# The second layer's score maximum from a difference and a positive part, and its denominator sum on one engine

## The chip, the cores and the metric

The kernel runs on one core of a Trainium2 chip. The metric is the device time of one execution in microseconds; lower is better. The engines are TensorE (PE in the profile, its weight loads PEld), VectorE (DVE), ScalarE (ACT), GpSimd (POOL) and SyncE (SP), which only issues transfers here.

## The reference

Two transformer layers over 2048 tokens of 128 features. The first has causal attention with 16 heads and a mixing by Fourier transforms; it is not touched. The second has a linear attention, not touched either, and then this attention over experts, with 8 heads, 5 experts and a head width of 64, of which the change touches the softmax:

```python
q = jnp.einsum('bthed,bthe->bhtd', q5, sd_g)
k = jnp.einsum('bthed,bthe->bhtd', k5, ss_g)
v = jnp.einsum('bthed,bthe->bhtd', v5, ss_g)
attn = jax.nn.softmax(jnp.einsum('bhid,bhjd->bhij', q * scale, k), axis=-1)
out = jnp.einsum('bhij,bhjd->bihd', attn, v)
o5 = jnp.einsum('bthd,dm->bthm', out, Wo).reshape(b, t, H, E, DIM)
return jnp.einsum('bthem,bthe->btm', o5, md)
```

`q5`, `k5`, `v5` are projections of the tokens per expert, `ss_g` and `sd_g` gates that keep the three best experts, `md` the mask of the three. Nothing is causal: each query sees 2048 keys.

## The kernel before

All work is written out by hand for each engine, with semaphores. The order of the second layer is one list, `SEQ1`, which `merge` makes from two: a foreground of 256 steps `u` (8 heads x 4 chunks of 512 queries x 8 pairs of key tiles), and a preparation of the next head whose items have a place in units of `u` (`preparation1`). Every engine walks this list and does its own part of each item, in order.

The foreground of a step is: `S`, TensorE computes the scores of two key tiles against a chunk of queries, transposed, into two PSUM banks (lines 775 and 776, two matmuls a tile: the second adds the fine part of the keys and, through a row of ones, minus the maximum of each query); ScalarE takes the exponential of both banks into `pbuf1` (line 960); two steps later `V` multiplies it with the values (line 786) and `D` adds it into the denominator sum `den`. `den` has 1024 columns; VectorE adds the first 704 of them (`SHARE`, line 1283; a copy in the first step of a chunk, line 1280), GpSimd the other 320 (lines 1383 and 1380). At the end of a chunk ScalarE copies the sum of products to `oT` (line 967), GpSimd adds the two halves of `den` (line 1388), TensorE folds and sums them (`F`, lines 797 and 802), VectorE divides (lines 1291 and 1292), and GpSimd multiplies with the expert mask into `onm` (line 1394) and adds that to `z` (line 1398). A step's exponential waits until the steps that used its buffer five steps ago are read.

The preparation of a head is: `w`, VectorE casts the weights (lines 1230 and 1231); `proj`, 48 projections of a token tile on TensorE (lines 747 to 749), each multiplied with the gates on VectorE (`gt`, line 1238) and, three of them together, summed over experts on GpSimd (lines 1367 to 1370), with two buffers for `gt`; `hi` and `lo`, the split into a coarse and a fine part (`sk1`, `sq1` by ScalarE, `sk2` and the rest of `sq1` by VectorE, lines 1250 and 1251); `t`, transposes (line 581) that ScalarE copies to `k1T`, `k2T`, `q1T`; and `max`: for each of 16 query tiles, four matmuls of 512 keys (line 759), each reduced by VectorE to one number a query (line 1256). `m` takes the largest of the four and its negative goes into `sq2`; `q2` transposes that into the row that `S` reads. So the maxima of a chunk must be done before its scores.

PSUM has eight banks. Four hold scores, one the products, and three (4, 5, 7) are the ring: `proj`, `max`, `F`, `y`, `t`, `q2` and `zt` take them in turn. `Ring` records for each item its turn and which engine reads it, and `take` lets TensorE write turn n only when turn n - 3 has been read:

```python
def take(ring, step):

    turn = ring.turn[step]
    if turn >= len(RING):
        wait_read(pe, ring, ring.order[turn - len(RING)])
    return ring.bank(step)
```

## Time and profile before

| what | value |
|---|---|
| median of three runs | 1859.26 us (1854.18 to 1868.14) |
| span of the profiled execution, from its first to its last instruction | 1857.2 us |
| busy TensorE, VectorE, ScalarE, GpSimd | 1645.3, 1435.4, 782.5, 878.0 us |
| mean granted TensorE clock | 0.945 of full |
| exponentials of the second layer, first to last start | 798.7 to 1823.7 us |

The profile gives the span of its execution; a time of that execution taken from outside is not given beside it, so the median, 2.1 us above the span, stands for what lies around it. Busy time is the time in which an engine has an instruction in flight. A matmul's end is modelled: at 512 columns it is recorded with some 390 ns while the next can start after 233. In a row, "idle before" is the time in which the engine stood, and the arrow names whom it waited for. A 4.0 us window of a full clock reads 1.00 under PEclk. Transfers play no part: the queues are busy 2% of the time.

### The profile page before, as it was taken

The page shows a single profiled execution, that of the slowest core. Times are in us where ns is not written, and L with a number is a line of the kernel's source. Part 1 is how long each engine was busy: PE and PEld are TensorE (multiplying, and loading weights), DVE is VectorE, ACT ScalarE, POOL GpSimd, SP SyncE. Part 2 cuts the span into 40 slices and gives each one's busy share as a digit, 9 for nine tenths or more (in the row PEclk, how much of TensorE's full clock was granted, in tenths as well). Part 3 has the DMA queues.
Part 4 walks back from the last instruction along what each step waited for, and adds up shares of the span by engine and source line. Part 5 has one row for each costly group of instructions (what it writes and reads, how often), then busy time and mean ns, then how long its engine had stood idle before and what let it go on. Part 6 is the DMA issues. An engine that isn't in the chain of part 4 may idle for free.

```text
span 1857.2 us, 26270 instructions
## 1 busy us (share of the span) xinstructions
PE 1645.3 (89%) x8612; PEld 999.3 (54%) x8612; DVE 1435.4 (77%) x2387; ACT 782.5 (42%) x1046; POOL 878.0 (47%) x906
## 2 busy tenths in 40 slices
PE   3899999999999672699899899899999899899997
PEld 2555555555554361566466466466565565565554
DVE  4996785785786369888888888888898888988862
ACT  3457557567556320223433434334334234234441
POOL 2710000000000024358678589589588587687654
PEclk9799999999999775889899999999999999999996
DMA  2000000000000000000000000000000000000000
GB/s 58 1 1 1 1 1 1 1 1 1 1 1 1 11 1 11 0 11 1 11 1 2 11 1 1 11 1 1 12 1 1 11 1 1 1 1 1 1 11 13
DMA packets 12224, 9.34 MB, mean 5 GB/s; under 512 B 3840, under 2 KB 11584, under 8 KB 12096
## 3 DMA queue, kind: packets, MB, share of 16 engines
q1 hardware_dynamic: 12096, 7.66, 1.5%
q8 instruction: 77, 1.26, 0.3%
q14 instruction: 51, 0.42, 0.1%
HBM read 6.61 MB, written 1.05 MB: 4 GB/s over the span
## 4 chain that ended last, share of the span: by engine, by line
PE 66%; DVE 19%; issue 7%; POOL 5%; ACT 2%; SPq 0%; DMA 0%; DVEq 0%; POOLq 0%; ACTq 0%
PE ps L786 10%; PE ps L606 8%; PE ps L623 7%; PE ps L638 7%; PE ps L759 6%; PE ps L581 5%; PE ps L775 4%; PE ps L776 4%; DVE den L1283 3%; PE ps L747 3%; DVE mxp L1256 3%; PE ps L749 2%; PE ps L748 2%; POOL z L1398 2%; PE ps L797 2%
## 5 line engine op out<-in xcount | busy, mean ns | idle before, releaser
L960 ACT ACTIVATE pbuf<-ps 128x1024 f32<-128x1024 f32 x256 | 262.1, 1024 | 524.0 <-PE ps L776 520.9
L1074 DVE TENSOR_REDUCE mxp<-ps 128x1 f32<-128x512 f32 (+3 forms) x560 | 354.2, 671 | 112.2 <-PE ps L606 56.2
L1256 DVE TENSOR_REDUCE mxp<-ps 128x1 f32<-128x512 f32 x512 | 342.5, 682 | 66.8 <-PE ps L759 66.1
L875 ACT ACTIVATE pbuf<-ps 128x1024 f32<-128x1024 f32 (+3 forms) x320 | 281.7, 896 | 199.1 <-PE ps L626 98.5
L1283 DVE TENSOR_TENSOR den<-den,pbuf 128x704 f32<-128x704 f32 x224 | 292.0, 1303 | 1.1
L786 PE MATMUL ps<-pbuf,h_v 128*64 128x512 f32 x1024 | 284.4, 634 | 0.0
L759 PE MATMUL ps<-k1T,q1T 128*128 128x512 f32 x512 | 223.4, 453 | 38.7 <-DVE mxp L1256 25.1
L1383 POOL TENSOR_TENSOR den<-den,pbuf 128x320 f32<-128x320 f32 x224 | 235.0, 1049 | 42.1 <-ACT pbuf L960 26.5
L606 PE MATMUL ps<-kM,qT 128*128 128x512 f32 (+3 forms) x640 | 243.6, 427 | 9.5 <-ACT kM L862 4.3
L1238 DVE TENSOR_TENSOR gt<-ps,gate 128x320 f32<-128x320 f32 x384 | 182.6, 484 | 54.8 <-PE ps L749 51.7
L623 PE MATMUL ps<-qT,kM 128*128 128x512 f32 (+3 forms) x640 | 207.7, 399 | 8.4 <-ACT pbuf L875 8.4
L775 PE MATMUL ps<-q1T,k1T 128*128 128x512 f32 x512 | 209.4, 409 | 2.3 <-ACT q2T L950 2.3
L776 PE MATMUL ps<-q2T,k2T 65*128 65x512 f32 x512 | 204.6, 400 | 0.0
L606 PEld LDWEIGHTS ps<-kM,qT 128*128 128x128 f32 x640 | 122.4, 197 | 118.7 <-DVE mxp L1074 88.7
L747 PE MATMUL ps<-wh,xh 128*128 128x320 f32 x384 | 136.1, 355 | 53.5 <-DVE gt L1238 36.9
L1367 POOL TENSOR_TENSOR gs<-gt 128x384 f32<-128x384 f32 x120 | 148.3, 1236 | 67.0 <-DVE gt L1238 65.3
L759 PEld LDWEIGHTS ps<-k1T,q1T 128*128 128x128 f32 x512 | 98.8, 194 | 146.3 <-DVE mxp L1256 87.0
L638 PE MATMUL ps<-pbuf,stagev 128*32 128x512 f32 (+3 forms) x1280 | 152.0, 547 | 0.0
L747 PEld LDWEIGHTS ps<-wh,xh 128*128 128x128 f32 x384 | 73.5, 191 | 142.1 <-DVE gt L1238 68.7
L1325 POOL TENSOR_SCALAR rstd<-meanvar 128x4 f32<-128x4 f32 x12 | 2.7, 227 | 304.5 <-DVE meanvar L995 304.5
L1340 POOL COPY stagev<-qkv 128x512 f32<-128x512 f32 x4 | 2.9, 722 | 288.8 <-PE ps L638 266.1
L623 PEld LDWEIGHTS ps<-qT,kM 128*128 128x128 f32 x640 | 117.9, 195 | 35.4 <-ACT pbuf L875 22.9
(212 smaller groups left out, 2484.3 us busy)
## 6 DMA issues: line engine op xcount, KB each, us to landing
wraw<-in_Wkv SPq DMA_DIRECT2D x16, 160.0 KB, 2.6
wraw<-in_Wq SPq DMA_DIRECT2D x8, 160.0 KB, 2.3
out<-x SPq DMA_DIRECT2D x4, 256.0 KB, 2.3
wqkv<-in_wqkvT SPq DMA_DIRECT2D x1, 192.0 KB, 4.0
masks<-in_masks SPq DMA_DIRECT2D x1, 128.0 KB, 4.1
dft<-in_dft SPq DMA_DIRECT2D x1, 128.0 KB, 2.3
wout<-in_Wo SPq DMA_DIRECT2D x2, 64.0 KB, 2.6
ident<-in_ident SPq DMA_DIRECT2D x1, 64.0 KB, 5.7
```

The costliest lines, as they stand in the source:

```text
L606: mm = pe.matmul(ps[:, bank, w * a:w * (a + 1)], qT[:, g % 2, P * it:P * (it + 1)], kM[g % 2][:, h + a, CH * b:CH * b + w], start=True, st ...
L623: mm = pe.matmul(ps[:, b, off:CH], kM[g % 2][:, h, P * jt:P * (jt + 1)], qT[:, g % 2, CH * c + off:CH * (c + 1)], start=True, stop=jt < TP ...
L638: mm = pe.matmul(ps[32 * h:32 * h + 32, ACC, off:CH], stagev[:, g % 2, jt, h, :], pbuf0[:, u % NP0, h % 2, off:CH], start=jt == 0, stop=jt ...
L747: pe.matmul(o, xh[:, t], wh[:, j, :], start=True, stop=False)
L759: pe.matmul(ps[:, bank, :], q1T[:, h % 2, P * it:P * (it + 1)], k1T[:, h % 2, CH * b:CH * (b + 1)], start=True, stop=True).then_inc(s_turn ...
L775: pe.matmul(ps[:, b, :], k1T[:, h % 2, t], q1T[:, h % 2, q], start=True, stop=False)
L776: mm = pe.matmul(ps[:, b, :], k2T[0:D1 + 1, h % 2, t], q2T[0:D1 + 1, h % 2, q], start=False, stop=True)
L786: mm = pe.matmul(ps[64 * i:64 * i + 64, ACC, :], h_v[:, h % 2, 2 * m + i, :], pbuf1[:, u % NP1, i, :], start=m == 0, stop=m == M1 - 1, til ...
L875: nc.scalar.activation(pbuf0[:, u % NP0, :, off:CH], ps[:, b:b + 2, off:CH], ACT.Exp, scale=float(D0) ** -0.5).then_inc(s_exp, 1)
L1074: v.tensor_reduce(mxp[:, i, h:h + n, b], ps[:, ring0.bank(step), 0:w * n].rearrange("p (h k) -> p h k", h=n), AX.X, ALU.max).then_inc(s_re ...
L1256: v.tensor_reduce(mxp1[:, it % TPC, b:b + 1], ps[:, ring1.bank(step), :], AX.X, ALU.max).then_inc(s_read1d, 1)
L1283: v.tensor_tensor(dn, dn, w, ALU.add).then_inc(s_den1, 1)
```

## The change

The maximum of two numbers a and b is b plus the positive part of a - b. Before, VectorE reduced the scores of each of four key chunks. Now the four form two pairs. GpSimd subtracts the keys of the second chunk of a pair from those of the first (`kd`, once a pair and head), TensorE multiplies the queries with `kd` (`dif`), ScalarE writes the positive part of that into one of two tiles `relu`, and TensorE multiplies with the second chunk's keys (`max`). VectorE then adds that bank and the tile and keeps the maximum in one operation, `tensor_tensor_reduce`, which writes the sum back into the tile. In the list, the difference of the next pair stands ahead of the maximum of this one. `dif` banks are read by ScalarE, `max` banks by VectorE; the number of matmuls and of turns is the same. A `relu` tile is free when VectorE has read the pair two before.

The denominator is added by VectorE alone, 1024 columns at a time; GpSimd only adds the two halves at the end of a chunk. The rest of the diff moves small tensors that only the linear attention and the gates use into space that is used again, and makes `sq2` narrower.

```diff
--- before.py
+++ after.py
@@ -44,6 +44,8 @@
+NR = 2
+LOW = -3e38
@@ -51,7 +53,6 @@
-SHARE = 704
@@ -103,10 +104,16 @@
             out += [(end + STAGE1[2] + 0.3 * w, ("t", h, c, w)) for w in range(3)]
+            if c % 2:
+                out.append((end + STAGE1[2] + 0.65, ("kd", h, c // 2)))
         for c in range(NC):
             end = u + M1 * c - MAX1
             start = end - M1 if c > 1 else u - MAX1 + 0.4 if c else u - U1 + PROJ1[1] + STAGE1[2] + 0.9
-            items = [("max", h, TPC * c + i, b) for i in range(TPC) for b in range(NC)]
+            pairs = [(h, TPC * c + i, p) for p in range(NC // 2) for i in range(TPC)]
+            items = [("dif", *pairs[0])]
+            for a, b in zip(pairs, pairs[1:] + [None]):
+                items += [("dif", *b)] if b else []
+                items.append(("max", *a))
@@ -410,7 +424,10 @@
-        ring1 = Ring(SEQ1, ("proj", "max", "F", "y"), ("t", "q2", "zt"))
+        ring1 = Ring(SEQ1, ("proj", "max", "F", "y"), ("t", "dif", "q2", "zt"))
@@ -752,12 +769,17 @@
-                elif kind == "max":
-                    _, h, it, b = step
+                elif kind in ("dif", "max"):
+                    _, h, it, p = step
                     bank = take(ring1, step)
                     wait_read(pe, ring1, ("t", h, NC - 1, 2))
-                    pe.matmul(ps[:, bank, :], q1T[:, h % 2, P * it:P * (it + 1)],
-                              k1T[:, h % 2, CH * b:CH * (b + 1)], start=True, stop=True).then_inc(s_turn1, 1)
+                    if kind == "dif":
+                        pe.wait_ge(s_kd, NC // 2 * h + p + 1)
+                        keys = kd[:, p, :]
+                    else:
+                        keys = k1T[:, h % 2, CH * (2 * p + 1):CH * (2 * p + 2)]
+                    pe.matmul(ps[:, bank, :], q1T[:, h % 2, P * it:P * (it + 1)], keys,
+                              start=True, stop=True).then_inc(s_turn1, 1)
@@ -944,6 +966,13 @@
+                elif kind == "dif":
+                    i = SLOT1[step[1:]]
+                    wait_turn(act, ring1, step)
+                    if i >= NR:
+                        wait_read(act, ring1, ("max", *PAIR1[i - NR]))
+                    nc.scalar.activation(relu[:, i % NR, :], ps[:, ring1.bank(step), :],
+                                         ACT.Relu).then_inc(s_read1a, 1)
@@ -955,7 +984,6 @@
-                        act.wait_ge(s_den1p, u - NP1 + 1)
@@ -1251,10 +1279,12 @@
                 elif kind == "max":
-                    _, h, it, b = step
+                    _, h, it, p = step
+                    above = relu[:, SLOT1[h, it, p] % NR, :]
                     wait_turn(dve, ring1, step)
-                    v.tensor_reduce(mxp1[:, it % TPC, b:b + 1], ps[:, ring1.bank(step), :],
-                                    AX.X, ALU.max).then_inc(s_read1d, 1)
+                    wait_read(dve, ring1, ("dif", h, it, p))
+                    v.tensor_tensor_reduce(above, ps[:, ring1.bank(step), :], above, 1.0, LOW, ALU.add, ALU.max,
+                                           accum_out=mxp1[:, it % TPC, p:p + 1]).then_inc(s_read1d, 1)
@@ -1272,7 +1302,7 @@
-                    w, dn = (a.rearrange("p a q -> p (a q)")[:, 0:SHARE]
+                    w, dn = (a.rearrange("p a q -> p (a q)")
                              for a in (pbuf1[:, u % NP1, :, :], den[:, mc % 2, :, :]))
@@ -1368,21 +1398,17 @@
+                elif step[0] == "kd":
+                    _, h, p = step
+                    wait_read(pool, ring1, ("t", h, 2 * p + 1, 0))
+                    if h:
+                        wait_turn(pool, ring1, ("dif", h - 1, NT - 1, p))
+                    a, b = (k1T[:, h % 2, CH * (2 * p + i):CH * (2 * p + i + 1)].bitcast(F32) for i in range(2))
+                    g_.tensor_tensor(kd[:, p, :], a, b, ALU.subtract).then_inc(s_kd, 1)
                 elif step[0] == "D":
                     u = step[1]
                     mc, m = u // M1, u % M1
-                    pool.wait_ge(s_exp1, u + 1)
-                    w, dn = (a.rearrange("p a q -> p (a q)")[:, SHARE:]
-                             for a in (pbuf1[:, u % NP1, :, :], den[:, mc % 2, :, :]))
...
-                        g_.tensor_tensor(dn, dn, w, ALU.add).then_inc(s_den1p, 1)
                     if m == M1 - 1:
-                        pool.wait_ge(s_den1p, u + 1)
                         pool.wait_ge(s_den1, u + 1)
```

The order on VectorE around the cast of a head's weights, before. `mxp` are the maxima, `den` the denominator, `wh` and `wl` the weights:

```order
L1291 RECIPROCAL rd<-ps 128x4
L1292 TENSOR_TENSOR on<-ps,rd 128x256
L1256 TENSOR_REDUCE mxp<-ps 128x1
L1230 CAST wh<-wraw 128x960
L1231 TENSOR_TENSOR wl<-wraw,wh 128x960
L1256 TENSOR_REDUCE mxp<-ps 128x1 x2
L1283 TENSOR_TENSOR den<-den,pbuf 128x704
L1256 TENSOR_REDUCE mxp<-ps 128x1 x3
L1283 TENSOR_TENSOR den<-den,pbuf 128x704
```

The same place after. The line numbers are those of the changed kernel; L1286 is the new operation, which is two instructions, the second of which writes the maximum:

```order
L1321 RECIPROCAL rd<-ps 128x4
L1322 TENSOR_TENSOR on<-ps,rd 128x256
L1286 ISA relu,mxp<-ps,relu 128x512
L1286 ISA mxp 128x1
L1258 CAST wh<-wraw 128x960
L1259 TENSOR_TENSOR wl<-wraw,wh 128x960
L1286 ISA relu,mxp<-ps,relu 128x512
L1286 ISA mxp 128x1
L1313 TENSOR_TENSOR den<-den,pbuf 128x1024
L1286 ISA relu,mxp<-ps,relu 128x512
L1286 ISA mxp 128x1
L1313 TENSOR_TENSOR den<-den,pbuf 128x1024
```

The weights stay where they were, between two maxima; around them half as many stand, and the denominator adds are wider.

The order on ScalarE in the same part of a head, before: `pbuf` are the exponentials, `q2T` the row with the maxima.

```order
L945 ACTIVATE q1T<-ps 128x512
L960 ACTIVATE pbuf<-ps 128x1024
L967 ACTIVATE oT<-ps 128x512
L960 ACTIVATE pbuf<-ps 128x1024 x6
L950 ACTIVATE q2T<-ps 1x512
```

After, with the exponential at L988 and the positive part at L974:

```order
L967 ACTIVATE q1T<-ps 128x512
L988 ACTIVATE pbuf<-ps 128x1024
L974 ACTIVATE relu<-ps 128x512 x2
L995 ACTIVATE oT<-ps 128x512
L988 ACTIVATE pbuf<-ps 128x1024
L974 ACTIVATE relu<-ps 128x512 x2
L988 ACTIVATE pbuf<-ps 128x1024
L974 ACTIVATE relu<-ps 128x512
L988 ACTIVATE pbuf<-ps 128x1024
L974 ACTIVATE relu<-ps 128x512 x2
```

One or two positive parts now stand between any two exponentials.

## Rows read from the trace of the kernel before

**Rows 1.** Page: busy tenths and granted clock in 40 slices of the span.
```profile
PE   3899999999999672699899899899999899899997
...
PEclk9799999999999775889899999999999999999996
```
**Rows 2.** Windows of one head and of the last head, all engines.
```profile
core 0: us, PE busy (x) PEld busy (x) DVE busy (x) ACT busy (x) POOL busy (x), PEclk, DMA share, GB/s
1193.20:1326.30 133.10, 123.30 (x593) 76.60 (x592) 113.85 (x171) 49.41 (x64) 101.52 (x108) 0.99 0.02 5
1719.60:1823.80 104.20, 101.61 (x460) 56.20 (x459) 77.10 (x104) 41.40 (x59) 62.44 (x45) 0.99 0.02 6
```
**Rows 3.** Waits of PE in the head 1193.2 to 1326.3: total, times, longest.
```profile
PE ps L759 <- DVE mxp L1256: 3.9, 1, 3.9
PE ps L747 <- DVE mxp L1256: 1.4, 1, 1.4
PE ps L759 <- DVE gt L1238: 1.3, 1, 1.3
PE ps L581 <- DVE sq L1251: 1.1, 1, 1.1
PE ps L581 <- DVE gt L1238: 0.7, 1, 0.7
PE ps L581 <- DVE mxp L1256: 0.5, 1, 0.5
```
**Rows 4.** Timeline around an add into z: start, duration, engine, what.
```profile
1212.09 2.93 POOL L1398 TENSOR_TENSOR z<-z,onm 128x1280 f32<-128x1280 f32 x1
1212.57 3.20 DVE L1283 TENSOR_TENSOR den<-den,pbuf 128x704 f32<-128x704 f32 x1
...
1216.43 0.41 PE L747 MATMUL ps<-wh,xh 128*128 128x320 f32 x1 [1.41 <-DVE mxp L1256]
```
**Rows 5.** Lines 1283 and 1238: shortest, median and longest in ns.
```profile
L1283 DVE TENSOR_TENSOR den<-den,pbuf x224: 874/1100/3407, 807.6 to 1832.5; 128x704 f32<-128x704 f32 x112
...
L1238 DVE TENSOR_TENSOR gt<-ps,gate x384: 471/482/493, 734.5 to 1684.9; 128x320 f32<-128x320 f32 x192
```
**Rows 6.** Timeline at the cast of the weights, and the window behind it.
```profile
1314.27 3.73 DVE L1231 TENSOR_TENSOR wl<-wraw,wh 128x960 fp32r<-128x960 f32 x1
...
1318.66 1.21 PE L759 MATMUL ps<-k1T,q1T 128*128 128x512 f32 x2 [3.92 <-DVE mxp L1256]
...
1319.00:1323.00 4.00, 3.90 (x9) 1.59 (x9) 4.00 (x7) 0.00 (x0) 2.90 (x3) 0.57 0.41 123
```
**Rows 7.** Groups of DVE in that head: busy, mean ns, idle before.
```profile
L1256 DVE TENSOR_REDUCE mxp<-ps 128x1 f32<-128x512 f32 x64 | 43.0, 682 | 7.2 <-PE ps L759 7.2
L1283 DVE TENSOR_TENSOR den<-den,pbuf 128x704 f32<-128x704 f32 x29 | 37.4, 1288 | 0.1
L1238 DVE TENSOR_TENSOR gt<-ps,gate 128x320 f32<-128x320 f32 x48 | 23.0, 484 | 7.1 <-PE ps L749 6.7 <-POOL h_v L1370 0.3
...
L1280 DVE COPY den<-pbuf 128x704 f32<-128x704 f32 x4 | 2.9, 718 | 0.0
```
**Rows 8.** Timeline of DVE, two small instructions.
```profile
1221.72 0.17 DVE L1269 TENSOR_SCALAR sq<-mx 128x4 fp32r<-128x4 f32 x1
1221.79 0.69 DVE L1256 TENSOR_REDUCE mxp<-ps 128x1 f32<-128x512 f32 x1
```
**Rows 9.** Timeline of DVE before the layer's first scores.
```profile
789.00 1.16 DVE L1231 TENSOR_TENSOR wl<-wraw,wh 128x960 fp32r<-128x960 f32 x1
790.08 4.27 DVE L1256 TENSOR_REDUCE mxp<-ps 128x1 f32<-128x512 f32 x7
```
**Rows 10.** Groups of POOL in the head 1193.2 to 1326.3.
```profile
L1383 POOL TENSOR_TENSOR den<-den,pbuf 128x320 f32<-128x320 f32 x28 | 29.1, 1039 | 6.0 <-ACT pbuf L960 4.4
...
L1388 POOL TENSOR_TENSOR den<-den 128x512 f32<-128x512 f32 x4 | 5.2, 1298 | 10.3 <-DVE den L1283 10.1
```
**Rows 11.** Groups of ACT over the span.
```profile
L960 ACT ACTIVATE pbuf<-ps 128x1024 f32<-128x1024 f32 x256 | 262.1, 1024 | 524.0 <-PE ps L776 520.9 <-DVE den L1283 2.2
...
L967 ACT ACTIVATE oT<-ps 128x512 f32<-128x512 f32 x32 | 19.2, 599 | 22.0 <-PE ps L786 21.8
```

More of the change, by code:

```diff
@@ L182, in build @@
         ones = sbuf(ctx, "ones", [P, 1])
-        wgate = sbuf(ctx, "wgate", [P, 2, H1 * E1])
         wout = sbuf(ctx, "wout", [P, 3, D])
-        wlin = sbuf(ctx, "wlin", [P, 4, D])
-        blin = sbuf(ctx, "blin", [P, 3, D])
-        bqcol = sbuf(ctx, "bqcol", [P, 1])
-        stdp = sbuf(ctx, "stdp", [P, 3, H0])
-        blockm = sbuf(ctx, "blockm", [P, D])
-        bd = sbuf(ctx, "bd", [P, 2, D])
-        bsum = sbuf(ctx, "bsum", [P, H0])
-        lden = sbuf(ctx, "lden", [P, 2, TPC, H0])
+        small = ExitStack()
+        sm = lambda name, shape, dt=F32: sbuf(small, name, shape, dt)
+        wgate = sm("wgate", [P, 2, H1 * E1])
+        wlin = sm("wlin", [P, 4, D])
+        blin = sm("blin", [P, 3, D])
+        bqcol = sm("bqcol", [P, 1])
+        stdp = sm("stdp", [P, 3, H0])
+        blockm = sm("blockm", [P, D])
+        bd = sm("bd", [P, 2, D])
+        bsum = sm("bsum", [P, H0])
+        lden = sm("lden", [P, 2, TPC, H0])
+        small.close()
+        relu = sbuf(ctx, "relu", [P, NR, CH])
+        kd = sbuf(ctx, "kd", [P, NC // 2, CH], F32R)
+        sq2 = sbuf(ctx, "sq2", [P, TPC, D1 + 1])
         l0 = ExitStack()
@@ L273, in build @@
         rd1 = s1("rd1", [P, TPC])
-        mxp1 = s1("mxp1", [P, TPC, NC])
+        mxp1 = s1("mxp1", [P, TPC, NC // 2])
         mx1 = s1("mx1", [P, TPC])
@@ L278, in build @@
         sq1 = s1("sq1", [P, TPC, P])
-        sq2 = s1("sq2", [P, TPC, P])
         k1T = s1("k1T", [P, 2, T], F32R)
@@ L340, in build @@
         s_st1 = sem("s_st1")
+        s_kd = sem("s_kd")
         s_m1 = sem("s_m1")
@@ L345, in build @@
         s_den1 = sem("s_den1")
-        s_den1p = sem("s_den1p")
         s_den1s = sem("s_den1s")
@@ L412, in build @@
         ring0 = Ring(SEQ0, ("max", "F", "pj", "mix", "lin"), ("k", "q", "q2", "at", "lt", "lt2"))
-        ring1 = Ring(SEQ1, ("proj", "max", "F", "y"), ("t", "q2", "zt"))
+        ring1 = Ring(SEQ1, ("proj", "max", "F", "y"), ("t", "dif", "q2", "zt"))
+        PAIR1 = [step[1:] for step in SEQ1 if step[0] == "dif"]
+        assert PAIR1 == [step[1:] for step in SEQ1 if step[0] == "max"]
+        SLOT1 = {pair: i for i, pair in enumerate(PAIR1)}
         def wait_read(eng, ring, step):
```

6 lines of the change are left out of this document (removed).

## The prediction

> **What bounds the kernel now.** I read the page first, then the second layer head by head in windows, then who TensorE waited for in one head, then the groups of instructions of that head, then short pieces of the timeline. The slices show two halves; the change touches only the second, from slice 16 on, where TensorE is at nine tenths at the full clock [rows 1]. The heads of the second layer repeat every 133.1 us, so one head stands for seven. In it TensorE is busy 123.3 us and VectorE 113.9 us at a granted clock of 0.99, which is its 2.4 GHz level; the last head, which projects nothing, takes 104.2 us with TensorE busy 101.6 [rows 2]. So the bound is TensorE, and what any relief of VectorE can give is TensorE's idle time: 133.1 - 123.3 = 9.8 us a head. Its waits say where it lies: 3.9, 1.4 and 1.3 us for banks that VectorE had not read, 1.1 + 0.7 + 0.5 = 2.3 us in front of the staging transposes (line 581), and two short ones for ScalarE that make up the rest [rows 3].
>
> The three large waits have causes that the timeline names. At 1212.57 a denominator add on VectorE took 3.20 us, against 874 ns for the shortest of its kind, because GpSimd's add into z ran from 1212.09 to 1215.02; TensorE stood until 1216.43 [rows 4, 5]. In the largest VectorE casts the next head's weights, and its second part, 3.73 us, stands behind another z; TensorE waited 3.92 us, and the four microseconds behind it ran at a granted clock of 0.57, near the 1.2 GHz level [rows 6].
>
> **The change part by part.** I work out VectorE's bill for a head first, since it decides whether VectorE stays behind TensorE, and then go through the waits.
>
> Maximum. Removed: 64 reductions of 682 ns [rows 7]. Consecutive ones overlap a little: the reduction at 1221.79 begins 0.07 after the instruction ahead of it, which lasts 0.17 [rows 8], so I count 0.08 us off each instruction: 64 x 0.60 = 38.4 us. Added: 32 instructions that add a PSUM bank to an SBUF tile of 512 columns and keep a maximum, each with a second one for the accumulator. No row has this operation. The nearest is the gate product (line 1238), also one PSUM and one SBUF input: 484 ns for 320 columns [rows 7]. Two additions of two tensors with nothing in their way give the slope: 874 ns at 704 columns [rows 5] and 1.16 us at 960 [rows 9], 1.1 ns a column. So 484 + 192 x 1.1 = 0.70 us. The accumulator instruction has one column; the small instructions at 1221.72 and 1221.79 bound it: 0.17 us as recorded, 0.07 to the next start [rows 8]. I take 0.12, the middle. 32 x (0.70 + 0.12 - 0.08) = 23.7 us, a saving of 14.7 us. Bounds: at 0.07 it is 16.3, and at double the time a column it is a loss (rival D).
>
> Whether the new instruction waits for GpSimd is a question of its own. The gate product never does: 384 of them lie between 471 and 493 ns while GpSimd is busy 101.5 of 133.1 us [rows 2, 5]. The addition with both inputs in SBUF waits: a mean of 1288 in this head against 874 [rows 5, 7]. The new one is of the first kind, so I charge nothing. By the Trainium skill, page "SBUF — State Buffer", section "Terms", VectorE and GpSimd share a port pair that one holds for a whole instruction while the other is blocked. Taken for every instruction that touches SBUF, it would put the mean wait of 0.41 us on each of the 32, 13 us a head, and eat the saving; the gate product speaks against that reading.
>
> Denominator. 28 additions grow from 704 to 1024 columns: 320 x 1.1 = 0.35 us, so 1.23 us alone. Their wait on GpSimd is 1288 - 874 = 0.41 us now. GpSimd loses its own 28 additions (29.1 us) and four copies (some 2 us) and gains two subtractions of 512 columns at 1298 ns: 101.5 - 31 + 2.6 = 73 us, 0.72 of before [rows 2, 10]. And the twin that always started on the same exponential is gone. I take 0.25 us (between 0.1 and 0.41). Each costs 1.48 instead of 1.29: 28 x 0.19 = +5.3 us, and the four copies, 718 ns now [rows 7], some +0.8 us. VectorE's sum: -14.7 + 5.3 + 0.8 = -8.6 us a head, 114 to about 105.
>
> ScalarE. 32 copies of the positive part, 128x512 from PSUM; the same shape takes 599 ns for oT, and the exponential 1024 [rows 11]: 19 us on 49 busy of 133 [rows 2]. They are hidden as long as a bank that holds a difference comes free in time. TensorE makes 132 turns of the three banks in a head (64 maxima, 48 projections, 12 + 4 transposes, 4 finals): 1.0 us a turn, and a bank is needed three turns later. A positive part behind an exponential is done after 1.02 + 0.60 = 1.6 us plus the matmul's 0.4. That is inside 3.0, so I take nothing. What if the cover fails is rival E. The orders show the positive parts between the exponentials; each is also held until VectorE has finished the pair two before it, and behind it the next exponential queues. TensorE needs that exponential only two steps later, about 8 us.
>
> TensorE itself keeps its 64 matmuls of 512 columns a head, half of them on kd. GpSimd's first subtraction of a head waits for the last matmul of the head before that reads the same half; behind it on GpSimd queue the expert sums of tile 12, and VectorE's gate products of tile 14 want those two tiles later. The GpSimd time freed pays for it; I charge nothing, and it is the reason for not crediting the staging waits in full.
>
> The waits, one by one. The cast (3.9 us): VectorE is still held behind GpSimd's z for the same 6 us, and what TensorE can do meanwhile grows by one 512-column matmul: -0.2. The low clock behind it stays. The two waits behind z (1.4 + 1.3): z still ends when it ended, the addition then takes 0.35 us more, the reader of the bank 0.14 more, and now and then the missing bank is one that ScalarE reads: 0, between -1.6 and +1.0. The staging waits (2.3): VectorE's splits come after a backlog that is now shorter: -1.5. The gaps too short to be listed: -0.5. Sum -2.2 us a head, seven heads -15.4.
>
> The start of the layer is different: before the first scores, 16 reductions and the weights' cast run one after the other; the last seven reductions take 4.27 us, 0.61 each, to 794.4 [rows 9], so sixteen take 9.8. Eight pairs at 0.74 on VectorE and two half-clock matmuls each, plus one fill through ScalarE, take some 3 us less (8 x 0.74 = 5.9 for VectorE, and the fill). The last head can save 0.5 of its 2.6 idle.
>
> Total -15.4 - 3 - 0.5 = -19 us. The profiled execution has a span of 1857.2 us, so about 1838; the median of the runs shown, 1859.26, lies 2.1 us above that span, so I forecast 1840 us, 1826 to 1850 for this case by itself. About 1% is what a measurement of this kernel can tell from no change, so it stands at the edge.
>
> **Rivals.**
> B, nothing to be seen: the staging waits hang on GpSimd's expert sums and not on VectorE's backlog, and only the start gains. For it: GpSimd at 101.5 us and the wait in front of its kd. Against: VectorE has no gap in the stretch ahead of the splits. 1855 us.
> C, more than forecast: every wait but the cast's goes, 9.8 - 3.9 = 5.9 us in seven heads is 41, with 3 at the start and 2.6 in the last head: 1859 - 47 = 1812 us. For it: each of these waits names VectorE. Against: z and the longer addition.
> D, slower: the new VectorE instruction runs at two cycles a column. Then it takes 0.70 + 512 x 1.1 = 1.26 us and with the accumulator 1.38, 32 x 1.30 = 41.6 against the 38.4 removed: +3.2, with the denominator +9.3 us a head, 123 of 133. VectorE is then as busy as TensorE; if half of it comes through, 4.6 x 7.7 heads = 35, 1894 us. It decides from about 1.0 us for the pair of instructions. For it: nothing in the trace has this operation. The Trainium skill, page "Vector Engine (DVE) Microarchitecture Reference", section "Points that are easy to get wrong", says that one kind of two-input instruction with an accumulator halves its rate when both inputs are wide and in SBUF; here one is in PSUM.
> E, slower too: the difference's bank is read late, because ScalarE sits behind an exponential and a pair that VectorE has not finished. From 3.0 us after the matmul on TensorE waits; 0.3 us in two pairs of three is 171 x 0.3 = 51 us, without the forecast's gain: about 1891 us. Against: ScalarE is busy 37%.
>
> **How the numbers follow.** A 0.46, B 0.28, C 0.10, D 0.09, E 0.07. The time is that of A, 1840. The range takes in C nearly whole and ends between B and D, 1808 to 1872, with D and E left out. Faster by over 1%: three quarters of A, all of C, a little of B: 0.47. Slower: most of D and E, 0.15. Within 1%: 0.38.
>
> **What would show it.** In the changed profile: the new line near 0.70 us with an accumulator row under 0.2; the denominator add at least 1.2 us, mean near 1.48; VectorE's busy time of a head near 105 us, GpSimd's near 73; heads 131 us apart; TensorE's wait behind the cast still 3.7 and its slow clock still there; the staging waits together under 1 us. The forecast is wrong if the head interval is under 128 (C), if TensorE waits on ScalarE's relu in many pairs (E), or if the new line is over 1 us (D).

## The result and the profile after

The changed kernel takes 1872.24 us (median of 4 runs, 1870.01 to 1875.51), beside 1858.97 us for the kernel before, timed along with it: a ratio of 1.0078, 95% interval 1.0042 to 1.0113. It is slower by 13.3 us, where 19 us less had been forecast, and lies just past the upper end of the range, 1872. Medians of the kernel before range from 1855.23 to 1858.97 us in this study, so each run's ratio is to the kernel before as timed along with it, and 3 us between runs timed apart say nothing.

First the page of the kernel after, answering to [rows 1]: busy time of each engine, and the slices of TensorE and of its granted clock.

```profile
span 1873.6 us, 26284 instructions
...
PE 1652.3 (88%) x8612; PEld 1004.2 (54%) x8612; DVE 1332.9 (71%) x2387; ACT 919.7 (49%) x1302; POOL 695.3 (37%) x666
...
PE   3799999999999662799899899999999899899997
...
PEclk9799999999999776899899999999999999899998
```

The slices say little here. TensorE's row has fewer eights in the heads than [rows 1] had, and the clock's row has one new eight, in slice 34 (counted from 0). What the page does show is that neither VectorE (71%) nor ScalarE (49%) has become the bound, and that TensorE's busy time grew, to 1652.3 us from 1645.3. The rest has to be read head by head.

Next one head from its first exponential to the next head's, and the last head, as windows (columns as in [rows 2]).

```profile
1202.80:1339.20 136.40, 125.13 (x593) 77.59 (x592) 100.39 (x171) 66.45 (x97) 79.40 (x78) 0.96 0.01 5
1742.40:1845.30 102.90, 99.02 (x447) 54.42 (x446) 68.88 (x100) 52.06 (x79) 30.50 (x12) 0.98 0.02 6
```

A head takes 136.4 us, 3.3 more than the 133.1 of [rows 2]. VectorE's busy time fell from 113.9 to 100.4, more than forecast (105). TensorE's busy time rose from 123.3 to 125.1 for the same 512-column products, and the granted clock fell from 0.99 to 0.96. So the head's 3.3 us are 1.8 more in which TensorE was busy and 1.5 more in which it stood (11.3 for 9.8). The work went away from VectorE as planned, and the head got longer.

The groups of VectorE, GpSimd and ScalarE over the span say what each edited instruction costs (columns as in [rows 7]).

```profile
L1313 DVE TENSOR_TENSOR den<-den,pbuf 128x1024 f32<-128x1024 f32 x224 | 340.8, 1522 | 2.6
...
L1286 DVE CUSTOM_DVE_ANT_0 relu<-ps,relu 128x512 f32<-128x512 f32 x256 | 175.2, 685 | 128.6 <-PE ps L781 128.4
...
L974 ACT ACTIVATE relu<-ps 128x512 f32<-128x512 f32 x256 | 151.4, 595 | 185.3 <-PE ps L781 119.0 <-DVE mxp L1286 65.5
...
L1286 DVE DVE_READ_ACCUMULATOR2_ANT mxp<- 128x1 f32 x256 | 21.0, 82 | 0.0
```

The new maximum is 685 ns and its accumulator 82 ns; 0.70 and 0.12 were forecast. The denominator add has a mean of 1522 ns; 1.48 was forecast. ScalarE's positive part is 595 ns as the forecast took it, and it is held behind VectorE for 65.5 us in all. The bill of VectorE was right. GpSimd's was not quite: its expert sums take longer.

```profile
L1398 POOL TENSOR_TENSOR gsum<-gs 128x192 f32<-128x192 f32 x120 | 106.3, 886 | 9.4
...
L1399 POOL TENSOR_TENSOR h_qk<-gsum,gt 128x128 f32<-128x128 f32 x120 | 78.1, 651 | 9.4
```

In the kernel before the same two groups had means of 644 and 549 ns. Each half of the change alone (e1 and e2 below) gives the first of them a mean of 741 and 726 ns, so VectorE's wider add is not all of it; which VectorE instruction they stand behind was not taken apart. Now the waits. TensorE's waits in the head 1202.8 to 1339.2 (us in total, times, longest), answering to [rows 3]:

```profile
PE ps L781 <- DVE mxp L1286: 3.7, 1, 3.7
PE ps L797 <- ACT q2T L979: 2.0, 2, 1.8
PE ps L764 <- DVE mxp L1286: 1.8, 1, 1.8
PE ps L781 <- DVE gt L1266: 1.6, 1, 1.6
PE ps L598 <- DVE gt L1266: 1.2, 1, 1.2
PE ps L764 <- DVE gt L1266: 0.6, 1, 0.6
```

Line by line: the cast's wait is 3.7 as forecast (3.9 before). The wait behind z grew from 1.4 to 1.8. The wait for a projection's bank read by the gate product grew from 1.3 to 1.6. The staging transposes no longer wait for VectorE's split (1.1 before), their wait for a gate product grew from 0.7 to 1.2, and TensorE now waits 1.8 for ScalarE's q2T. The sum of what is listed went from 8.9 to 10.9, where 2.2 less had been forecast. Part of that is in waits too short for either list: all of TensorE's standing grew by 1.5. The head grew by 3.3 us, so the waits aren't all.

The place behind z shows the rest. The timeline of GpSimd, VectorE and TensorE there, and windows behind the wait and behind the cast's wait, answer to [rows 4] and [rows 6].

```profile
1216.17 2.35 POOL L1420 TENSOR_TENSOR onm<-on,maskd 128x1280 f32<-128x1280 f32 x1 [1.11 <-DVE on L1322]
1218.60 2.94 POOL L1424 TENSOR_TENSOR z<-z,onm 128x1280 f32<-128x1280 f32 x1
...
1218.91 3.71 DVE L1313 TENSOR_TENSOR den<-den,pbuf 128x1024 f32<-128x1024 f32 x1
1222.54 0.68 DVE L1286 CUSTOM_DVE_ANT_0 relu<-ps,relu 128x512 f32<-128x512 f32 x1
...
1223.28 0.42 PE L764 MATMUL ps<-wh,xh 128*128 128x320 f32 x1 [1.78 <-DVE mxp L1286]
...
1224.59 1.97 PE L808 MATMUL ps<-pbuf,h_v 128*64 128x512 f32 x4
...
1222.80:1228.80 6.00, 5.52 (x19) 3.25 (x20) 4.90 (x10) 1.51 (x2) 5.15 (x8) 0.72 0.00 0
1324.80:1332.80 8.00, 4.75 (x10) 2.33 (x11) 6.77 (x9) 2.11 (x3) 1.56 (x1) 0.57 0.19 62
```

VectorE's add began 0.31 us after z and took 3.71 us against 3.20 before; TensorE stood 1.78 us for the reader behind it. Then came something that was not there before: four numerator matmuls took 1.97 us, where the same four take 1.08 at full clock, and six microseconds ran at a granted clock of 0.72. After the 1.41 us wait of [rows 4] the clock had stayed at 2.4 GHz (a window from 1216.40 to 1222.40 of the kernel before reads 1.00). At the cast the low stretch is longer too: eight microseconds at 0.57. I count a low stretch as its length times (1 - granted clock): 6.00 x 0.28 + 8.00 x 0.43 = 5.1 us in this head. Before it was 4.00 x 0.43 = 1.7 us [rows 6]. The count is an upper bound of what a stretch costs, since a slow clock takes nothing while TensorE stands: the stretch at the cast begins 2 us before the wait there ends. So the difference, 3.4 us, is not the whole of the 3.3 us by which a head grew; it overlaps with the waits, and what the clock costs by itself has to be measured (below).

The whole span can now be summed. The first exponential of the layer comes 1.7 us earlier (797.0 for 798.7), the seven heads from there take 945.4 us instead of 924.0 (+21.5 before rounding), the last head 102.8 instead of 101.1 (+1.7), and what follows the last exponential takes 28.4 us instead of 33.4 (-5.0): together +16.5, as the spans say (1873.6 and 1857.2, +16.4 as rounded). The piece at the end is clock too. Windows behind the last exponential, of the kernel before and then of the kernel after:

```profile
1823.70:1829.00 5.30, 5.30 (x19) 2.48 (x19) 0.83 (x2) 1.45 (x3) 2.70 (x4) 0.50 0.00 0
```

```profile
1845.20:1850.00 4.80, 4.80 (x27) 2.37 (x24) 1.42 (x2) 1.99 (x5) 0.00 (x0) 1.00 0.00 0
```

The kernel before had a low clock there (0.50), the kernel after none. The same clock that cost the heads gave this back.

### The profile page after: what moved, and what is told of

It is laid out like the page before. It is cut to its first block, busy times and chain, and to the rows that moved or that the text cites. A ratio compares the mean times of both kernels' runs of the same rounds, so it can differ in the third digit from the quotient of the medians.

```text
span 1873.6 us, 26284 instructions
## 1 busy us (share of the span) xinstructions
PE 1652.3 (88%) x8612; PEld 1004.2 (54%) x8612; DVE 1332.9 (71%) x2387; ACT 919.7 (49%) x1302; POOL 695.3 (37%) x666
## 4 chain that ended last, share of the span: by engine, by line
PE 66%; DVE 13%; POOL 9%; issue 7%; ACT 4%; SPq 0%; DMA 0%; DVEq 0%; ACTq 0%; POOLq 0%
PE ps L808 10%; PE ps L623 8%; PE ps L655 7%; PE ps L640 6%; PE ps L781 6%; PE ps L797 5%; PE ps L798 4%; PE ps L598 4%; PE ps L764 3%; POOL z L1424 3%; POOL onm L1420 2%; PE ps L766 2%; PE ps L765 2%; PE ps L819 2%; DVE mxp L1102 2%
## 5 line engine op out<-in xcount | busy, mean ns | idle before, releaser
L988 ACT ACTIVATE pbuf<-ps 128x1024 f32<-128x1024 f32 x256 | 261.9, 1023 | 258.8 <-PE ps L798 257.0
L1313 DVE TENSOR_TENSOR den<-den,pbuf 128x1024 f32<-128x1024 f32 x224 | 340.8, 1522 | 2.6
L808 PE MATMUL ps<-pbuf,h_v 128*64 128x512 f32 x1024 | 288.9, 644 | 0.0
L1286 DVE CUSTOM_DVE_ANT_0 relu<-ps,relu 128x512 f32<-128x512 f32 x256 | 175.2, 685 | 128.6 <-PE ps L781 128.4
L974 ACT ACTIVATE relu<-ps 128x512 f32<-128x512 f32 x256 | 151.4, 595 | 185.3 <-PE ps L781 119.0
L1397 POOL TENSOR_TENSOR gs<-gt 128x384 f32<-128x384 f32 x120 | 144.3, 1203 | 149.2 <-DVE gt L1266 147.6
L781 PE MATMUL ps<-kd,q1T 128*128 128x512 f32 x256 | 111.4, 441 | 26.7 <-DVE mxp L1286 23.4
L781 PE MATMUL ps<-k1T,q1T 128*128 128x512 f32 x256 | 118.2, 463 | 11.4 <-DVE gt L1266 11.0
L1420 POOL TENSOR_TENSOR onm<-on,maskd 128x1280 f32<-128x1280 f32 x32 | 75.9, 2371 | 133.5 <-DVE on L1322 133.5
L797 PEld LDWEIGHTS ps<-q1T,k1T 128*128 128x128 f32 x512 | 100.1, 195 | 44.4 <-ACT pbuf L988 18.5
```

The source lines that it names most:

```text
L781: pe.matmul(ps[:, bank, :], q1T[:, h % 2, P * it:P * (it + 1)], keys, start=True, stop=True).then_inc(s_turn1, 1)
L797: pe.matmul(ps[:, b, :], k1T[:, h % 2, t], q1T[:, h % 2, q], start=True, stop=False)
L808: mm = pe.matmul(ps[64 * i:64 * i + 64, ACC, :], h_v[:, h % 2, 2 * m + i, :], pbuf1[:, u % NP1, i, :], start=m == 0, stop=m == M1 - 1, til ...
L988: nc.scalar.activation(pbuf1[:, u % NP1, :, :], ps[:, b:b + 2, :], ACT.Exp, scale=float(D1) ** -0.5).then_inc(s_exp1, 1)
L1313: v.tensor_tensor(dn, dn, w, ALU.add).then_inc(s_den1, 1)
```

## The experiments

Two readings had to be told apart first (called W and S in what was on record): the wide add on VectorE is the whole loss, or the way through ScalarE is. Each half of the change was therefore run alone.

**e1: the new maximum, with the denominator split again.** The edit to the kernel after ("..." marks lines left out):

```
+SHARE = 704
...
-w, dn = (a.rearrange("p a q -> p (a q)")
+w, dn = (a.rearrange("p a q -> p (a q)")[:, 0:SHARE]
...
+g_.tensor_tensor(dn, dn, w, ALU.add).then_inc(s_den1p, 1)
...
```

> The changed kernel with the denominator split again as before (VectorE 704 columns, GpSimd 320); the maximum by difference stays. Theory W (the wider denominator add is the whole loss: behind GpSimd's add into z it ends later, TensorE waits longer and its clock falls): the head interval goes from 136.4 back to 133 us or less, the wait at line 764 is 1.4 us or less and the clock behind it stays at 1.00, total 1845 us (1838 to 1855), ratio to the kernel before 0.99. Theory S (the path through ScalarE, with its positive parts held until VectorE has finished the pair two before, is the loss): the interval stays near 136 us, total 1865 to 1875, ratio 1.005.

Measured: 1880.57 us, ratio 1.0118 (1.0074 to 1.0163).

**e2: the kernel before, with the whole denominator sum on VectorE.** The edit, to the kernel before, is the reverse one: the split at SHARE, GpSimd's add and the waits for its semaphore go.

> The kernel before with the whole denominator sum on VectorE; the maxima stay 64 reductions a head. VectorE then has about 10 us more a head than before the change, 123 of 133. Theory W: slower than the changed kernel, since it has the wide add and not the relief: 1885 us (1870 to 1910). Theory S: the wide add is harmless, about 1859 to 1866 us, ratio 1.00.

Measured: 1885.78 us, ratio 1.0145 (1.0100 to 1.0190).

W had e2 right (1885) and e1 wrong (1845); S had e1 slower, though not by enough (1865 to 1875), and e2 wrong (1859 to 1866). So neither stands as it was put. Each half alone is slower than the kernel before, by 24.3 and 29.5 us (1856.25 beside them), and both are slower than the two together. Costs of two parts that simply add cannot do that. What the two have in common is in the windows, one of a head of each, the longest or as long as any, and then its low stretches:

```profile
1342.00:1481.80 139.80, 128.38 (x593) 79.77 (x592) 95.95 (x171) 66.56 (x97) 104.01 (x110) 0.94 0.02 4
1362.00:1368.00 6.00, 5.83 (x21) 3.73 (x22) 4.61 (x11) 1.53 (x3) 5.69 (x10) 0.72 0.00 0
1444.00:1452.00 8.00, 6.86 (x22) 4.31 (x23) 4.37 (x4) 3.24 (x6) 6.40 (x7) 0.57 0.01 2
1468.00:1476.00 8.00, 5.67 (x13) 2.59 (x15) 5.38 (x10) 2.56 (x4) 5.82 (x5) 0.57 0.20 61
```

```profile
1202.50:1342.60 140.10, 129.76 (x593) 79.24 (x592) 118.19 (x170) 49.30 (x64) 75.84 (x76) 0.94 0.01 4
1222.50:1226.50 4.00, 3.46 (x9) 1.36 (x9) 3.79 (x6) 0.00 (x0) 3.72 (x6) 0.58 0.00 0
1262.50:1268.50 6.00, 5.24 (x17) 3.34 (x18) 5.38 (x10) 0.63 (x2) 5.69 (x8) 0.72 0.01 3
1328.50:1340.50 12.00, 11.28 (x28) 5.42 (x30) 9.49 (x16) 1.97 (x2) 0.00 (x0) 0.57 0.14 41
```

By the same count e1's head has 1.7 + 3.4 + 3.4 = 8.5 us of low clock, and e2's 1.68 + 1.68 + 5.16 = 8.5. TensorE's busy time is 128.4 and 129.8 us for the same work that took 123.3. VectorE is at 96 us in the one and at 118 in the other, and both heads take 140 us: VectorE's load doesn't rank them. These are the worst heads. From the second to the sixth, heads of e1 take 135.8 to 139.8 us and those of e2 136.2 to 140.1, and the low clock in them is 3.4 to 8.5 us. Over the seven heads e1 takes 952.2 us with 40.8 of low clock and e2 952.4 with 36.7, the kernel after 945.4 with 34.0 and the kernel before 924.0 with 14.6: more low clock goes with longer heads, and taken off it leaves 909 to 916.

**e3: the kernel after, with onm and z on GpSimd in four instructions of 320 columns each.**

```
...
-g_.tensor_tensor(z[:, tiles], z[:, tiles], onm[:], ALU.add).then_inc(s_z, 1)
+for i in range(TPC):
+    n = TPC * c + i
+    ins = g_.tensor_tensor(z[:, n], z[:, n], onm[:, i], ALU.add)
+ins.then_inc(s_z, 1)
```

> The changed kernel with GpSimd's product into onm and its add into z each in four instructions of 320 columns in place of one of 1280. Theory W: VectorE's add no longer stands behind the whole add of 2.9 us but behind one quarter of it, 0.75 us; the longest denominator add falls from 3.7 to about 2 us, TensorE's waits of 1.8 and 1.6 us and the low clock behind the first go: 2.5 to 3.5 us a head, total 1850 us (1843 to 1858); GpSimd has some 0.6 us more per chunk. Theory S: no change beyond 3 us, 1868 to 1875.

Measured: 1882.53 us, ratio 1.0126 (1.0086 to 1.0165). TensorE's waits in the head 1195.7 to 1330.0:

```profile
PE ps L764 <- DVE gt L1266: 4.7, 2, 2.7
PE ps L797 <- ACT q2T L979: 3.9, 2, 3.7
PE ps L598 <- DVE gt L1266: 1.2, 1, 1.2
```

What was expected on the spot came: the longest denominator add fell from 3.7 to 1.9 us, and the waits behind z and behind the cast are gone. In their place are 2.7 us for a gate product and 3.7 us for q2T. The pieces together take longer on GpSimd (z: 4 x 1277 ns = 5.1 us against 3.1). The seven heads took 938.3 us, 7 less than in the kernel after and not the 17 to 25 that had been expected, and the last head lost 12.5 us: TensorE's waits for z in it went from 3.9 us to 12.7. A run that moves a delay says little about its price.

A third `relu` tile was to show what ScalarE's hold behind VectorE costs. It doesn't fit into SBUF beside the kernel's other tensors, so no run shows that.

**The clock by itself.** To take the low stretches away without touching what a wait hangs on, I put matmuls that nothing reads (fillers) in front of the step that waits. They write a score bank that is free then, and fill the time in which TensorE would stand:

```
...
+pe.wait_ge(s_exp1, u)
+for _ in range(n):
+    pe.matmul(ps[:, 2 * ((u + 1) % NS), :], q1T[:, h % 2, 0:P], k1T[:, h % 2, 0:CH],
+              start=True, stop=True)
```

What the other engines do to release TensorE isn't changed.

> The changed kernel, with idle matmuls that nothing reads (512 columns, into the score bank that is free) put in front of two steps of TensorE in each head: 6 before the projection that waits 1.78 us behind the GpSimd product, and 13 before the score difference that waits 3.7 us behind the expert cast. The waits themselves keep their length. Clock theory (the time is lost in the stretches of low granted clock that follow the waits): the windows behind both waits show 1.0 instead of 0.57 and 0.50, a head takes about 133 us instead of 136.4, and the kernel takes 1845 to 1855 us. Rival (the waits themselves, or work on VectorE, ScalarE and GpSimd, set the head's time, and the clock only shows that TensorE has time): head and total stay within 1 us and 8 us of those of the changed kernel, or get worse by the added matmuls.

Measured: 1858.07 us, ratio 0.9994 (0.9976 to 1.0012), against 1872.24 without them. The place behind z in this run:

```profile
1210.93 3.70 DVE L1337 TENSOR_TENSOR den<-den,pbuf 128x1024 f32<-128x1024 f32 x1
...
1213.36 1.53 PE L769 MATMUL ps<-k1T,q1T 128*128 128x512 f32 x6
1215.29 0.41 PE L788 MATMUL ps<-wh,xh 128*128 128x320 f32 x1 [0.40 <-DVE mxp L1310]
...
1216.17 1.08 PE L832 MATMUL ps<-pbuf,h_v 128*64 128x512 f32 x4
...
1194.80:1328.10 133.30, 126.92 (x612) 80.96 (x611) 100.22 (x171) 66.28 (x96) 79.49 (x78) 0.99 0.02 5
1254.80:1258.80 4.00, 4.00 (x15) 3.56 (x14) 3.31 (x7) 0.09 (x1) 3.84 (x6) 0.57 0.00 0
```

From the start of VectorE's add to the projection it is 1215.29 - 1210.93 = 4.36 us here and 1223.28 - 1218.91 = 4.37 in the kernel after: the wait is the same. The numerators behind it take 1.08 instead of 1.97. A head takes 133.3 instead of 136.4. So the clock theory holds for 14 of the kernel's microseconds, though the time missed the 1845 to 1855 us expected. In the head shown one low stretch was left, behind a wait of 1.6 us that had no filler, and which was followed by full clock in the kernel after. Even inside this run it comes and goes: the next head, from 1328.1, has the same wait of 1.6 us and no low stretch, and takes 133.0 us for 133.4.

> The kernel before, with 14 such idle matmuls in each head in front of the maximum's matmul that waits 3.9 us behind the expert cast. Clock theory: the one low stretch of a head goes, a head takes 1 to 1.7 us less than 133.1, and the kernel 1846 to 1852 us. Rival (the clock follows the load and costs nothing here): the kernel stays within 4 us of the kernel before.

Measured: 1855.90 us, ratio 0.9989 (0.9972 to 1.0005). By itself this can't be told from no change, and it lies within the 4 us that the rival gave. The heads say more: from the second to the sixth, two took 132.1 us and three 133.7; in those of 133.7 the drop had moved behind the staging wait of 1.1 us, which the heads of 132.1 have as well. So here a low stretch costs 1.6 us of a head.

> The changed maximum with the denominator sum split at column 704 as before, and idle matmuls in front of three steps: 5 at the GpSimd product, 13 at the cast, 9 before the scores that wait for the staged queries (2.8 us). Clock theory: the low stretches, worth 8 us of a head of 139.8, go; a head takes 132 to 134 us, and the kernel 1830 to 1850 us. Rival (the waits and the queue of ScalarE set the head's time): a head stays above 138 us and the kernel above 1870 us.

Measured: 1847.93 us, ratio 0.9942 (0.9923 to 0.9961), against 1880.57 without fillers. The second to sixth heads are 132.0 us at a granted clock of 1.00, the seven together 920.6 where e1 had 952.2. This kernel is the fastest of the study and beats the kernel before as well as the one after.

**The four kernels at full clock.** With that, the two halves of the change can be priced without the clock of the heads. Fillers stand at the long waits of a head in each; none stand ahead of the first scores or behind the last.

> The kernel before with idle matmuls in front of four of TensorE's waits of each head (4 at the wait of 1.4 us behind GpSimd's product, 4 at the one of 1.25 us for a projection's bank, 3 at the staged queries, 14 at the cast), so that no stretch of low clock is left. Theory (low stretches add to the head, each about 1.6 us, and everything else stays): every head takes 132.1 us, where the earlier kernel with idle matmuls at the cast alone had 132.1 and 133.7 by turns, and the kernel 1846 to 1850 us. Rival: idle matmuls at short waits push TensorE's own work back, and the kernel stays at 1856 us or above.

> The whole denominator sum on VectorE alone, with idle matmuls at the same four waits (5, 5, 3, 14). Clock theory: a head takes 131.5 to 133 us instead of 140 and the kernel 1846 to 1854 us, so that at full clock the wide sum costs a head less than 1 us. Rival (VectorE's wider sum holds the head up by itself): a head takes over 134 us and the kernel over 1860 us.

> The changed kernel with idle matmuls at four waits (6 at GpSimd's product, 5 at the wait of 1.6 us for a projection's bank, 5 at the staged queries, 13 at the cast), where w1 had them at the first and the last and kept one low stretch of a head. Clock theory: that stretch goes too, a head takes 131.6 us, and the kernel 1842 to 1850 us. Rival: a head stays at 133.3 us and the kernel at 1858 us, its waits being the cost.

Measured: w4 1852.13 us (ratio 0.9966, 0.9947 to 0.9985), w5 1873.66 us (1.0070, 1.0042 to 1.0097), w6 1856.41 us (0.9976, 0.9955 to 0.9997). One head of w3, w4, w5 and w6, in this order:

```profile
1191.10:1323.10 132.00, 127.51 (x620) 81.20 (x619) 95.08 (x171) 66.46 (x96) 105.68 (x110) 1.00 0.02 5
```

```profile
1189.30:1321.50 132.20, 127.65 (x619) 80.65 (x617) 113.22 (x171) 49.48 (x65) 101.59 (x108) 1.00 0.02 5
```

```profile
1197.50:1332.60 135.10, 128.99 (x620) 80.87 (x619) 117.61 (x171) 49.43 (x65) 75.12 (x76) 1.00 0.02 4
```

```profile
1192.00:1325.00 133.00, 128.54 (x622) 81.25 (x621) 100.23 (x171) 66.54 (x97) 79.42 (x78) 1.00 0.02 5
```

All four have a clock of 1.00 (column PEclk), so what differs between these heads is not the clock. As a table, with the kernels without fillers beside them (seven heads: from the layer's first exponential to the last head's first; each from one profiled execution; low clock by the count above, over the seven heads):

| maximum, denominator | with fillers, us | head, us | seven heads, us | without fillers, us | seven heads, us | low clock in them, us |
|---|---|---|---|---|---|---|
| before, split (w4; before) | 1852.13 | 132.1 | 920.1 | 1858.97 | 924.0 | 14.6 |
| new, split (w3; e1) | 1847.93 | 132.0 | 920.6 | 1880.57 | 952.2 | 40.8 |
| before, whole (w5; e2) | 1873.66 | 135.2 | 939.9 | 1885.78 | 952.4 | 36.7 |
| new, whole (w6; after) | 1856.41 | 133.0 | 926.3 | 1872.24 | 945.4 | 34.0 |

In the seven heads with fillers, the new maximum gains nothing beside the split sum (+0.5 us) and 13.7 us beside the whole one; the whole sum costs 5.7 us with the new maximum and 19.8 with the old one. The change as a whole is +6.2 us in the heads.

The fillers gave back 3.9 us of the seven heads of the kernel before, 31.6 of e1's, 12.5 of e2's and 19.1 of the kernel after's. That is 0.27 to 0.77 of the low clock counted, so the count goes with the length of the heads but is no price.

The kernels' times show 4.2 us in favour of w3 against w4, but that isn't the new maximum's. Start, heads and last head of w3 together take 0.7 us more than w4's; what is shorter is the piece behind the last exponential, where no filler stands. The windows from there to the end, of w4 and then of w3:

```profile
1817.30:1850.80 33.50, 24.18 (x97) 15.54 (x95) 4.54 (x12) 5.26 (x16) 9.22 (x7) 0.60 0.06 16
```

```profile
1818.00:1846.70 28.70, 19.38 (x97) 13.26 (x95) 4.92 (x12) 5.27 (x16) 10.51 (x8) 0.74 0.06 18
```

The same 97 matmuls take TensorE 24.18 us at a granted clock of 0.60 and 19.38 at 0.74; the longest wait, for z, is 6.2 us in both. The drop fell there in w4, as in the kernel before, and not in w3. Nor does the old maximum bring it: w2 has that too and takes 29.8 us there. For the same reason the times of w6 and w4 differ by 4.3 us (1854.06 to 1858.25 against 1850.21 to 1855.74) and not by 6.2.

w4's time, 1852.13 us, lies between its theory's (1846 to 1850) and its rival's (1856 or more), with the expected head of 132.1. w5's expectation failed, since its head is 135.2 and not under 133; its rival's figures came. The whole sum on top of the old maximum has a cost of its own, the waits in front of the staging transposes: 1.8 us for gate products and 1.2 for a maximum, against 0.7 and 0.5 in w4. Up to 0.7 us of a head in w5 may be the price of three fillers at a wait that had gone, an estimate from 3 x 0.233 us. Fillers do cost where nothing waits: the seventh head has no cast, w4 runs its 14 there all the same, and that head takes 130.2 us against 127.0 in the kernel before. w6's own expectation (131.6 us a head, 1842 to 1850) was missed too: the low stretch left in w1 cost only 0.4 us of a head (133.4 against 133.0 there) and not 1.7. The head that has it lacks a wait of 0.6 us for a gate product that the next one has; what absorbed the rest was not traced.

**w7: one place alone.** The kernel after, with only the six fillers behind z.

> The changed kernel with the 6 idle matmuls behind GpSimd's product alone. The places add if each low stretch costs only its own time: 136.4 less 1.6 is 134.8 us for a head, 1859 to 1862 us for the kernel. If the stretches depend on each other (a gap filled here moves the drop to the next wait), a head takes 136 us or more, the kernel over 1866 us.

Measured: 1877.13 us, ratio 1.0086 (1.0058 to 1.0113): nothing gained at all, as the second reading had it. Its waits are those of the kernel after, and behind z the clock is now 1.00. The low clock came back elsewhere. TensorE's q2T wait and the window behind it, in the kernel after and then in w7:

```profile
1305.85 0.47 PE L797 MATMUL ps<-q1T,k1T 128*128 128x512 f32 x1 [1.79 <-ACT q2T L979]
...
1306.00:1312.00 6.00, 5.69 (x30) 3.19 (x30) 1.40 (x2) 4.44 (x8) 2.51 (x2) 1.00 0.01 3
```

```profile
1304.99 0.47 PE L819 MATMUL ps<-q1T,k1T 128*128 128x512 f32 x1 [1.79 <-ACT q2T L1001]
...
1305.00:1311.00 6.00, 6.00 (x24) 3.36 (x24) 1.54 (x2) 2.72 (x5) 2.50 (x2) 0.72 0.00 0
```

The same wait of 1.79 us is followed by 1.00 in one kernel and by 0.72 in the other. The length of a wait, then, doesn't tell by itself whether the clock falls behind it. The places don't add: with one filled, the drop came at another.

**w8 and w9: the queue of ScalarE.** The q2T copy stands on ScalarE behind the copy of the staged keys (line 955), which waits 1.7 us for GpSimd's h_v. Listing that copy later was to free it. The edit, the same in both:

```
-STAGE1 = (2.2, 3.0, 3.7)
+STAGE1 = (2.9, 3.0, 4.2)
```

> The changed kernel, with ScalarE's copy of the staged queries and keys listed after its copy of the max queries (and the transposes half a step later); no idle matmuls. Theory (the 1.8 us wait of TensorE for q2T is the queue of ScalarE, where the copy stands behind one that waits 1.7 us for GpSimd's expert sums): the q2T wait falls under 0.5 us, a wait of 0.5 to 1.5 us for the staged queries stays, a head takes 134 to 136 us and the kernel 1855 to 1870 us. Rival (the copy only moves, and the wait for the staged queries grows by as much): the kernel stays within 5 us of 1872.

Measured: 1876.53 us, ratio 1.0112 (1.0084 to 1.0141), within 5 us of 1872, as the rival had it.

> The new maximum with the split denominator sum, the later staging copy, and idle matmuls at GpSimd's product (5), at a projection's bank (3), at the staged queries (3) and at the cast (13). Theory: as w3 (1848 us, 132.0 us for a head), less the 1.4 to 2 us of a head that the queue of ScalarE held: 130 to 131.5 us for a head, 1836 to 1845 us. Rival (the wait is elsewhere): 1846 to 1852 us.

Measured: 1904.88 us, ratio 1.0259 (1.0232 to 1.0286). TensorE's waits in a head of w8 and then of w9:

```profile
PE ps L781 <- DVE mxp L1286: 3.6, 1, 3.6
PE ps L781 <- DVE gt L1266: 3.4, 3, 1.6
...
PE ps L797 <- ACT q2T L979: 0.6, 2, 0.4
```

```profile
PE ps L811 <- DVE gt L1297: 4.0, 3, 1.8
PE ps L827 <- ACT q2T L1009: 2.6, 2, 2.4
```

In w8 the q2T wait did fall, from 2.0 to 0.6 us, as the theory of the queue said. The waits of the maximum's matmuls for gate products rose from 1.6 to 3.4 and took it back. w9's heads are 139.9 to 143.1 us from the second to the sixth, and its expectation was wrong by 60 us. It differs from w3 in the places of its fillers as well as in the list, and low clock came back (6.8 to 3.4 us a head), so no cause is shown for it. The edit moves all four chunks' staging, not only the one at the head's end, and I didn't try one for that chunk alone.

## Why the prediction was wrong

**What held.** The pair of instructions on VectorE: 0.70 + 0.12 us forecast, 0.685 + 0.082 measured, so rival D fell. The denominator add: 1.48 forecast, 1522 ns. GpSimd's head of 73 us came out at 79, VectorE's 105 at 100. The cast's wait: 3.7 forecast and measured. Rival E named the wrong harm: ScalarE's positive part is held behind VectorE, 9.5 us of a head, but no matmul waited over 0.2 us for it. (E's sum is off as well: without the forecast's gain it gives 1859 + 51 = 1910 us; 1891 keeps the gain.) The start of the layer gave 1.7 of the 3 us: the first exponential at 797.0 instead of 798.7.

The last head was to gain 0.5 us and lost 1.7.

**What failed, the first step.** "The two waits behind z (1.4 + 1.3): ... 0, between -1.6 and +1.0". Both grew, from 1.41 to 1.78 and from 1.25 to 1.58: +0.7 us, within the bounds that the text gave. The terms that it had named (0.35 for the wider add, 0.14 for the reader) did not go into the sum, and they are what came: the add behind z took 3.71 us for 3.20. The relief that was to offset them didn't come; z still held VectorE there.

**The second step.** "The staging waits (2.3): ... -1.5". The transposes' own waits fell from 2.3 to 1.2 us, but their wait for a gate product rose in that from 0.7 to 1.2, and a new one of 1.79 us, which the sum had not, ends the chain h_v on GpSimd, copy on ScalarE, q2T. w8, which took the copy out of the way, took that wait away, as that chain asks; rival B, which hung the staging on GpSimd's expert sums, had that part right. The transposes' wait doesn't follow GpSimd's load: it is 0.7 in w3 with GpSimd busy 106 us of a head, and 1.2 in w6 with 79. At full clock the whole change is then +0.9 us a head (w6 against w4), where -2.2 had been summed: an error of 3.1 us a head, some 22 in seven.

**The third, and the one that made it slower.** "The low clock behind it stays", taken as a constant, so that the sum had no term for the clock. It went from 1.7 to 5.1 us in a head. Runs w4 and w6 price it over the seven heads: 924.0 us in the kernel before against 920.1 in w4, 945.4 in the kernel after against 926.3 in w6. So taking the low clock away gives the one 3.9 us and the other 19.1, and 15.3 of the 21.5 us that the heads grew are clock. Fillers that no wait covers cost some 3 us in the seventh head of both w4 and w6 (14 or 13 of 0.233 us, an estimate), so each price is low by about that and the difference stands. The other 6.2 us are there at full clock, and the waits of the two steps above are where they show. For the same heads -15.4 had been forecast, so of the error of 36.9 us in them 15.3 is the clock and 21.6 the waits. Without the clock the forecast would still have been wrong, and the kernel's time no shorter than before.

The Trainium skill, page "TensorE: Matmul & The Clock Gate", section "Part 1: The HAM clock gate (the "warmup" mystery)", says that a monitor sets TensorE's clock by how busy it has been of late. w1 agrees: matmuls that nothing reads brought 0.72 back to 1.00 behind an unchanged wait on VectorE. The page adds that the monitor's periods run free of the program, so that the point of a change varies. That would let one and the same wait go either way, as w7 shows of the 1.79 us one and w1 of the 1.6 us one from head to head; no run here shows the periods themselves.

What stays open: behind which wait the clock falls. w7 and w1 show that the length of the wait alone doesn't decide it. Open too is what makes the whole sum with the old maximum so dear at full clock (19.8 us in the heads); its waits are named above, but no run took them away one by one.

## What to carry to other kernels

Where TensorE is the bound and the trace shows a low granted clock behind one of its waits, the sum of a change needs a term for the clock: behind a wait that grew by 0.4 us came a low stretch that counts 1.7 us, and over the heads the clock took 15.3 us. A low stretch costs less where TensorE has waits to absorb it: 1.6 us of a head in w2, 0.4 in w1. Judge a part of such a change with fillers at the waits, in all variants alike, and by the stretch that has them; without them, e1 made the new maximum look 28 us dear in the heads, where w3 and w4 show it to cost nothing. What has no fillers can still mislead: the tail gave w3 its 4 us over w4. Fillers that nothing reads, at every long wait and not at one, are also a small gain that can be kept: with 25 of them a head the kernel before takes 1852.13 us, 0.3% less, and the new maximum with the split sum and 27 of them 1847.93 us, 0.6% under the kernel before.

## What the runs showed of the hardware

The operation that adds two tensors and keeps the maximum, one input in PSUM and one in SBUF at 512 columns, takes 685 ns and 82 ns for its accumulator, with a mean that GpSimd's work doesn't raise (684 and 685 ns in w1 and w3, whose GpSimd was busy 79 and 106 us of a head). The addition of two SBUF tiles of 1024 columns does wait: 3.71 us beside z against 1.21 at its shortest. And TensorE's four numerator matmuls take 1.97 us in the low stretch and 1.08 at 2.4 GHz: the added time comes behind the wait, in other lines than the one that waited, so a list of waits alone doesn't show it.
